# One extra product behind each fill, an earlier copy of weights, and an earlier table load in a four-layer convolution kernel on Trainium2

## What is computed

```
x = x + relu(batchnorm(deform_conv(norm(x))))      # layer 0, offsets and mask from 3x3 convolutions
x = x + sign_conv(norm(x))                         # layer 1, 1x1: sign(x).w + x.sign(w)
x = x + deform_conv(norm(x))                       # layer 2, offsets from a 3x3 convolution
x = x + attention(norm(x))                         # layer 3: f1, f2, f3 = 1x1 convolutions with bias,
                                                   # softmax(f1^T f2) over 4096 keys, times f3, plus norm(x)
```

## Time and profile before

| | us |
|---|---|
| median of 3 runs | 1315.96 |
| lowest, highest | 1315.5, 1316.31 |
| the profiled execution, by its device time | 1317.74 |
| its span, first to last instruction | 1315.0 |
| TensorE busy | 1166.4 |
| VectorE busy | 1011.4 |
| ScalarE busy | 661.8 |
| GpSimd busy | 484.8 |
| mean granted TensorE clock, share of 2.4 GHz | 0.945 |

### The profile page before, as it was taken

The page is one execution under the profiler, slowest core; times in us unless marked ns, Lnnn a source line. Parts: engine busy times, 40 slices in busy tenths (PEclk is TensorE's granted clock), DMA queues, the critical chain, the costliest instruction groups (busy, mean ns, idle before and its releaser), DMA issues.

```text
span 1315.0 us, 20260 instructions
## 1 busy us (share of the span) xinstructions
PE 1166.4 (89%) x7066; PEld 490.1 (37%) x7126; DVE 1011.4 (77%) x1679; ACT 661.8 (50%) x882; POOL 484.8 (37%) x537
## 2 busy tenths in 40 slices
PE   4899997586999999978898888888998999999996
PEld 1788884143444443422232322222222222222221
DVE  8799998894766566668879888888766777777772
ACT  4877675644554455322343444444655444444453
POOL 4000000037777777777777777772000000000000
PEclk9999997697999999956799999999999999999999
DMA  2654450048544442111111111110000000000000
GB/s 53 138 131 112 120 103 1 0 127 234 157 124 131 140 151 69 52 47 49 51 54 50 52 51 51 50 50 22 1 1 1 8 9 0 0 0 0 0 1 16
DMA packets 59672, 79.21 MB, mean 60 GB/s; under 512 B 12230, under 2 KB 43974, under 8 KB 59414
## 3 DMA queue, kind: packets, MB, share of 16 engines
q1 hardware_dynamic: 44342, 47.03, 13.6%
q0 software_dynamic: 15264, 31.29, 8.4%
HBM read 70.94 MB, written 7.34 MB: 60 GB/s over the span
## 4 chain that ended last, share of the span: by engine, by line
PE 67%; DVE 21%; issue 5%; ACT 4%; DMA 1%; DVEq 1%; SPq 0%; ACTq 0%; another core or an unknown queue 0%
PE psum L1831 15%; PE psum L1966 12%; PE psum L1948 9%; PE psum L1989 8%; PE psum L1716 6%; DVE maxes L1143 5%; DVE quads L372 3%; PE psum L1731 3%; DVE probs_and_weighted L881 3%; PE psum L1914 3%; PE psum L1743 2%; PE psum L1841 2%; PE psum L1803 2%; PE psum L1995 2%; DVE probs_and_weighted L891 2%
## 5 line engine op out<-in xcount | busy, mean ns | idle before, releaser
L554 POOL DMA_INDIRECT tile_data<-quad_table,index_u x477 | 470.0, 985 | 409.2 <-DMA quad_table<-quad_rows_or_splits 260.7
L1143 DVE TENSOR_REDUCE maxes<-psum 128x1 f32<-128x512 f32 x512 | 329.1, 683 | 98.9 <-PE psum L1948 92.1
L1573 ACT ACTIVATE quads<-psum 128x1024 f32<-128x1024 f32 x256 | 248.1, 1021 | 260.7 <-PE psum L1995 241.5
L1966 PE MATMUL psum<-quads 128*64 128x512 f32 x1024 | 267.0, 616 | 7.1 <-DVE maxes L1143 6.9
L1831 PE MATMUL psum<-scratch,quad_rows_or_splits 128*128 128x512 f32 (+1 forms) x486 | 209.1, 571 | 20.8 <-DVE scratch L966 19.2
L1989 PE MATMUL psum<-quads,probs_and_weighted 32*128 32x512 f32 x1024 | 146.9, 643 | 3.5 <-issue 2.1
L1831 PEld LDWEIGHTS psum<-scratch,quad_rows_or_splits 128*128 128x128 f32 x486 | 87.8, 192 | 117.1 <-issue 101.2
L1948 PE MATMUL psum<-products_or_attention 128*128 128x512 bf16 x226 | 83.8, 414 | 42.6 <-DVE maxes L1143 37.5
L978 DVE TENSOR_TENSOR probs_and_weighted<-psum,quads 128x512 f32<-128x512 f32 (+1 forms) x81 | 51.5, 643 | 79.3 <-PE psum L1831 74.1
L1432 ACT ACTIVATE vals<-psum 96x384 f32<-96x384 f32 x53 | 25.8, 487 | 144.3 <-PE psum L1795 144.3
L1966 PEld LDWEIGHTS psum<-quads 128*64 128x64 f32 x1024 | 55.4, 136 | 107.2 <-issue 100.0
(11 more groups left out here) (226 smaller groups left out, 1431.3 us busy)
## 6 DMA issues: line engine op xcount, KB each, us to landing
products_or_attention<-positions SPq DMA_DIRECT2D x30, 576.0 KB, 8.0
products_or_attention<-bands SPq DMA_DIRECT2D x12, 768.0 KB, 7.6
tile_data<-quad_table,index_u POOLq DMA_INDIRECT x477
quads<-bands SPq DMA_DIRECT2D x6, 768.0 KB, 10.7
quad_table<-quad_rows_or_splits SPq DMA_DIRECT2D x4, 768.0 KB, 9.1
products_or_attention<-bands SPq DMA_DIRECT2D x4, 576.0 KB, 8.4
quad_table<-quad_rows_or_splits SPq DMA_DIRECT2D x2, 640.0 KB, 8.5
products_or_attention<-positions SPq DMA_DIRECT2D x4, 288.0 KB, 6.8
```

What stands on the lines that cost most here:

```text
L554: pool.indirect_dma_start(out=out[:, k * CORNERS * C:(k + 1) * CORNERS * C], out_offset=None, in_=table, in_offset=bass.IndirectOffsetOnAx ...
L1143: v.reduce_max(maxes[:, c // NBLK, c % NBLK:c % NBLK + 1], psum[:, FREE + c % 2, :], AXIS_X)\
L1573: act.activation(probs[:, s % 2, 2 * BLK * h:2 * BLK * (h + 1)], psum[:, SCORES + 2 * h:SCORES + 2 * h + 2, :].rearrange("p a n -> p (a n) ...
L1966: last = pe.matmul(psum[2 * C * h:2 * C * h + 2 * C, SUMS, :], f3[b][:, 4 * s + i, :], probs[:, s % 2, BLK * i:BLK * i + BLK], start=s == ...
```

## The change

It has five pieces.

1. The upper halves of the quads have 34 rows, the lower ones 30, in both deformable layers.
2. ScalarE copies the weights of tile 0 ahead of the first hats. The wait ahead of it is for the indices of image 0 alone.
3. ScalarE loads the table with the square root after layer 1's tanh and sign, ahead of `take_sums`.
4. A new function `keep_warm` on TensorE multiplies a bf16 identity by four copies of itself into bank `SUMS`; nobody reads the result.
5. It is called behind each of the 16 fills of image 0's preparation. Fills of image 0 inside the attention, and all fills of image 1, have none.

```diff
-        TOP = H // 2 + 1
+        TOP = H // 2 + 2
         HALVES = ((0, TOP), (TOP, H))
...
                 act.preload_act_table(ACT.Abs)
                 act.wait_ge(rows_copied, 9 * B)
+                act.wait_ge(indexed, 1)
+                take_weights(0).then_inc(first_weights, 1)
                 hats_of_bands(0, -1)
                 hats_of_bands(1, 0)
-                act.wait_ge(indexed, B)
-                take_weights(0).then_inc(first_weights, 1)
...
             for b in range(B):
                 l1_tanh_and_sign(b)
+            act.preload_act_table(ACT.Sqrt)
             take_sums()
...
+            def keep_warm():
+
+                pe.matmul(psum[:, SUMS, :].rearrange("p (m n) -> p m n", m=4), ident_h[:, :],
+                          ident_h[:, None, :].to_broadcast([P, 4, P]), start=True, stop=True)
...
                 for n in fills:
                     fill(0, n)
+                    keep_warm()
```

## The result

The changed kernel takes 1308.96 us (median of 4 runs, 1305.88 to 1309.69), the kernel before 1316.02 on the same chip: ratio 0.9944, 95% interval 0.9928 to 0.996. It is faster by some 7 us, where I forecast no change that could be measured (1317.2). The profiled execution took 1309.69 us, span 1307.9.

What follows compares the result with a forecast made beforehand. TensorE was busiest (1166 of 1315 us), but no engine was full everywhere, so each stage was priced by its owner. 0 - 1.28 - 2.2 + 4.7 = +1.2 us on the median 1315.96 gave 1317.2 us, range 1309 to 1319.6.

Steps and rivals of the forecast that it cites:

- Upper halves of 34 rows: Quad writes of both deformable layers: 0.067 us a row, growth repaid by shorter lower halves; cost 0, at worst +0.2 per layer.
- Table load: ScalarE ahead of layer 2: square-root table load at 246.05 us moves into an earlier idle gap; -1.28 us.
- Weights ahead of hats: Start of the dense stage: selection 0 and TensorE start 8.8 us early, most lost later; -2.2 us, bounds -6 and +0.3.
- the load of step 3: Dense stage: ScalarE gets x of step 3 at 319.21 us regardless, since that load is issued behind the stores.
- The stall of 4.7 us: Dense stage: TensorE waits for ScalarE's values ahead of tile 0's convolution, resuming at 327.35; 3.1 of 8.8 us are left.
- The slower rival: Behind the stall at tile 0's convolution: 8 us of half clock eat the start's gain; +3.7 us, 1319.7 us, chance 0.13.
- The sixteen products: Image 0's preparation: 11 products in the chain at 0.43 us each, clock staying at half; +4.7 us.
- the second rival: Image 0's preparation: products hide or the clock rises at tile 3; 1313.7 us, chance 0.13.
- the bound of 0.615: Image 0's preparation: us per added product at half clock if nothing overlaps, making the products' upper bound +6.8 us.
- Their weights load beside the fill before: Image 0's preparation: the added products' weight loads overlap the preceding fill, leaving 0.43 us for each product.
- That the products raise the clock: Image 0's preparation: full clock holds through the fills until GpSimd's gathers bind, 3.2 us won; 1309.3 us, chance 0.20.
- my sum: Whole kernel: 0 - 1.28 - 2.2 + 4.7 = +1.2 us, counted as no change.

## Why the prediction was wrong

**The step that failed is the first, "Upper halves of 34 rows", at cost 0.** It took 0.067 us a row from the two shapes of the earlier trace rows and carried it over to 34 and 30 rows. Both shapes have odd counts, so the slope was right for odd counts alone, as the run with 35 rows shows (2595 and 2196 ns; the old slope gives 2595 and 2195). In its place: 1.06 us less for each of layer 2's ten writes and some 0.9 for each of layer 0's, 10.5 us earlier from the dense stage on in the trace, 9.9 us of the time by the medians. No rival held this case either, and the bounds were 0 and +0.2: two rows of the very operation seemed near enough to need no other. The trace of before had the warning, in VectorE's groups by shape over the whole span:

```profile
L1053 DVE TENSOR_SCALAR quad_rows_or_splits<-x_state,norm 32x1024 f32<-32x1024 f32 x6 | 4.8, 802 | 0.1
...
L1085 DVE TENSOR_SCALAR conv_sums_or_normed<-x_state,norm 32x4096 f32<-32x4096 f32 x1 | 2.6, 2578 | 0.0
```

The same operation on 32 partitions, on 4096 elements, takes 2578 ns, and the quad write on 2112 elements took 2461. (2578 - 802) / 3072 = 0.58 ns per element, against 0.067 us / 64 = 1.04. VectorE was at half its rate in the quads.

**Table load, -1.28: right.** The lead grows from 1.62 us at the root's statistics to 2.91 at the first quad write of layer 2. The load shows at 234.74 us, before 241, and was not made again. The figure of the Trainium skill, "ScalarE: Activation LUTs", section "What ACT_TABLE_LOAD costs", 2.66 us with a drain, would give more. No drain stands in these rows either, so the sum by it does not hold here.

**Weights ahead of hats, -2.2: right in its mechanism, and by the medians in its size.** They give 2.1 us (0.7 to 3.5 by the interval). In the trace the lead was 10.2 us at selection 0 and not 8.8, since the first bands landed 1.6 us earlier, at 295.42, and 3.8 remained. I had the load of step 3 come at 319.21 "whatever happens"; it came at 317.38 in that run and at 317.60 in the run with the products alone, so it does move from one execution to the next. The stall of 4.7 us came out as 3.84 and 3.72. With this edit alone the convolution behind it ran at half clock (1.49 us), as forecast; in the changed kernel it did not (0.84), and the clock fell only behind it. The slower rival, half clock for 8 us, did not happen: 3.4 us of it in the changed kernel, 6.8 in the run with this edit alone.

**The sixteen products, +4.7: the mechanism right, the price mis-sized.** The clock stayed at 0.50 from the first fill to 609.6 us, past tile 4, so the second rival did not happen either. Up to tile 4 the chain of waits contains 12 products and not 11: all three of tile 2 are in it. Together they cost 8.1 us, 0.67 each on average and not 0.43, above even the bound of 0.615. Between two key fills the price of one is 0.84, as the last of a tile ahead of the convolution 0.54. The words that failed are "Their weights load beside the fill before": I let the weights of the product and of the fill behind it load for nothing, as in the earlier trace rows between products of one kind. Here both loads start with their own products, and the change from an f32 fill to a bf16 product and back costs 0.40 beyond the columns. That the loads are all of the 0.40 was not tested.

**The rivals.** That the products raise the clock did not happen with one per fill; its second half, gathers that bind once the rest is faster, did, in the runs that came to tiles 4 to 7 early. The time it gave, 1309.3, is that of the result by chance: some -10 from the halves and +8 from the products had no place in it. With my sum corrected by the sizes of the traces (-10.5, -1.3, -3.8, +8.1) comes -7.5 us, with the medians of the halves and the weights in place of theirs (-9.9, -2.1) comes -5.2; -7.1 was measured. The sum closes within the 2 us by which medians and single traces differ here.

## What to carry to other kernels

Two durations of one operation give a slope only for shapes of the same kind: before pricing a size, divide every group of that operation in the trace by its elements, and where two differ twofold look for a parity or a stride before the size. Cut VectorE's one-source SBUF work into even numbers of rows, and then look at what GpSimd does beside it. Work that is added to hold a clock has to be priced with the change of weights on both sides of it, and a lead won upstream is worth only what the slowest feeder downstream (here GpSimd's gathers) leaves of it.

## What the runs showed of the hardware that was not expected

- VectorE's f32 TENSOR_SCALAR between SBUF tiles: 33 ns for a row of 64 elements where the number of rows is even, 66 to 67 where it is odd (eight counts from 28 to 36).
- Beside the even writes GpSimd's short instructions take up to 1.1 us longer (a memset 1.32 us and not 0.21), beside odd ones they don't (0.21 with 33 and with 35 rows). In the kernel before, the issue of a gather beside VectorE's write of one run of 4096 elements (2.58 us, L1085) takes 2.62 us and not 0.94.
- TensorE at 1.2 GHz: a bf16 product between two f32 fills of 33 rows costs its columns plus 0.40 us, of which 0.11 stand in the product and the rest in the fill behind it.
- The clock in products of 33 rows: it fell 0.5 us into them even after 4.27 us of gap-filling products, and with four full-height products behind each fill it first rose 39 us after they began, and fell three times more. The Trainium skill, "TensorE: Matmul & The Clock Gate", Part 1, has sustained activity release the throttle; these runs agree for full-height work without gaps (the band products of the changed kernel began at 289.28 us at 0.50, and the clock rose at 292.2) and not for thin fills with one product of full height behind each, which stayed at 0.50 from 556 us until past 600.
